# Masked attention stage: normalising the probabilities before they are turned, instead of dividing the heads' output by sums from a product with ones

## What is computed

```python
def _L0_xattn_ref(query, keys, values, mask, Wq, bq, Wk, bk, Wv, bv, Wo, bo):
    q = (query @ Wq.T + bq).reshape(N, Lq, HEADS, HEAD_DIM).transpose(0, 2, 1, 3)
    ...
    energy = jnp.einsum('bhqd,bhkd->bhqk', q, k)
    energy = jnp.where(mask[:, None, None, :] == 0, jnp.float32(-1e+20), energy)
    attention = jax.nn.softmax(energy / np.sqrt(HEAD_DIM), axis=-1)
    out = jnp.einsum('bhqk,bhkd->bhqd', attention, v)
    out = out.transpose(0, 2, 1, 3).reshape(N, Lq, EMBED)
    return out @ Wo.T + bo
x = x + _L0_xattn_ref(_layernorm(x), ctx_1024, ctx_1024, mask_BxS2_ik0, ...)
```

## Time and profile before

| | us |
|---|---|
| median of 3 runs (3192.03 to 3195.54) | 3193.3 |
| profiled execution | 3187.25 |
| its span, first to last instruction | 3185.5 |
| busy over the span: TensorE matmul | 3017.8 |
| VectorE | 2186.4 |
| ScalarE | 2009.2 |
| GpSimd | 941.1 |

### The profile page before, as it was taken

One profiled execution on the slowest core, in us unless ns is written; L12 is line 12 of the kernel. 1 busy time (PEld: TensorE's weight loads), 2 busy tenths in 40 slices (PEclk: granted clock), 3 DMA queues, 4 the chain that ended last, 5 costly groups with the idle time before them and its releaser, 6 DMA issues. The chain is left out here.

```text
span 3185.5 us, 88343 instructions
## 1 busy us (share of the span) xinstructions
PE 3017.8 (95%) x34369; PEld 2466.6 (77%) x34369; DVE 2186.4 (69%) x5188; ACT 2009.2 (63%) x3697; POOL 941.1 (30%) x812
## 2 busy tenths in 40 slices
PE   8999999979999999999979999999999999799999
PEld 7888888857877877877868888788788787564798
DVE  5777777766666666666644788778778877567543
ACT  5777777757767767677743677676666766332444
POOL 3444444337656555555630000000000000111210
PEclk9999999989999999999989999999999999899899
DMA  2111111237888888888885111111111110552000
GB/s 86 47 46 46 46 46 46 57 52 128 151 141 150 151 137 146 152 145 148 156 188 173 35 42 49 55 42 49 56 42 42 54 36 19 179 163 77 7 21 27
DMA packets 643036, 273.37 MB, mean 86 GB/s; under 512 B 549387, under 2 KB 617952, under 8 KB 642736
## 3 DMA queue, kind: packets, MB, share of 16 engines
q1 hardware_dynamic: 613168, 225.13, 33.6%
q10 hardware_dynamic: 29568, 44.05, 4.2%
HBM read 113.37 MB, written 21.50 MB: 42 GB/s over the span
## 5 line engine op out<-in xcount | busy, mean ns | idle before, releaser
L1310 POOL TENSOR_TENSOR front_parts<-wide_prob,front_parts 128x1024 f16<-128x1024 f32 x256 | 549.1, 2146 | 377.5 <-ACT front_parts L1536 318.6
L1629 DVE TENSOR_REDUCE wide_row_max<-wide_score 128x1 f32<-128x1024 f32 x256 | 312.6, 1221 | 167.4 <-PE wide_score L1348 166.5
L1348 PE MATMUL wide_score<-wide_kT,wide_qT 128*128 128x512 f32 x1536 | 414.3, 405 | 4.9 <-ACT wide_prob L1524 3.3
L1524 ACT ACTIVATE wide_prob<-wide_score,wide_neg_max 128x1024 f32<-128x1024 f32 x256 | 285.2, 1114 | 157.3 <-DVE wide_neg_max L1632 151.0
L886 ACT ACTIVATE mask_prob<-mask_prob,mask_row_min 128x256 f32<-128x256 f32 x512 | 232.0, 503 | 161.7 <-DVE mask_row_min L966 161.7
L1348 PEld LDWEIGHTS wide_score<-wide_kT,wide_qT 128*128 128x128 f32 x1536 | 277.5, 190 | 66.0 <-issue 8.9
L1536 ACT ACTIVATE front_parts<-wide_prob 128x1024 f16<-128x1024 f32 x256 | 269.8, 1054 | 16.8 <-ACT wide_prob L1524 8.3
L2472 DVE TENSOR_REDUCE cell_row_max<-cell_score 128x8 f32<-128x512 f32 x192 | 131.0, 682 | 148.5 <-PE cell_score L2097 146.6
L117 POOL TENSOR_TENSOR cell_var_eps<-cell_mean_var,const_eps 128x4 f32<-128x4 f32 x8 | 1.6, 202 | 651.9 <-DVE cell_mean_var L111 651.9
L1364 PE MATMUL wide_turn<-front_probT,wide_v 128*128 128x256 f16 x1536 | 189.5, 273 | 2.5 <-DMA front_probT<-front_parts 2.5
L1364 PE MATMUL wide_pv<-front_probT,wide_v 128*128 128x256 f16 x1536 | 189.9, 273 | 0.5 <-DMA front_probT<-front_parts 0.5
(11 more groups left out here) (364 smaller groups left out, 6845.6 us busy)
## 6 DMA issues: line engine op xcount, KB each, us to landing
cell_w_stage<-cell_weights ACTq DMA_DIRECT2D x24, 768.0 KB, 6.1
mask_ctx<-in_ctx SPq DMA_DIRECT2D x32, 512.0 KB, 3.9
ctx_ctx<-in_ctx SPq DMA_DIRECT2D x32, 512.0 KB, 4.2
mask_mask<-in_mask_BxS_ik SPq DMA_DIRECT2D x32, 256.0 KB, 4.0
front_probT<-front_parts SPq DMA_TRANSPOSE x512, 3.2
cell_w_stage<-in_L_ffn_We ACTq DMA_DIRECT2D x24, 256.0 KB, 2.7
cell_w_stage<-in_L_ffn_Wo ACTq DMA_DIRECT2D x24, 256.0 KB, 3.1
front_x_all<-in_x SPq DMA_DIRECT2D x32, 128.0 KB, 2.0
```

The costliest lines, as they stand in the source:

```text
L1310: pool.tensor_tensor(parts[:, s % 2, LO, :], prob[:, s % 2, :], parts[:, s % 2, HI, :], ALU.subtract).then_inc(part_lo, 1)
L1348: mm = pe.matmul(score[:, s % 2, half * 512:(half + 1) * 512], qT[:, u_par, a, s * P:(s + 1) * P], kT[:, par, b, half * 512:(half + 1) * 5 ...
L1524: act.activation(prob[:, s % 2, :], score[:, s % 2, :], ACT.Exp, bias=neg_max[:, s % 2:s % 2 + 1], scale=SHARP, accum_out=row_sum[:, u_par ...
L1629: dve.tensor_reduce(row_max[:, one], score[:, s % 2, :], AX.X, ALU.max).then_inc(max_found, 1)
```

## The change

What it does, part by part:

1. ScalarE's exponentials write their row sums (`accum_out`) to `row_sum`. VectorE inverts the two sums of a step as soon as its exponentials are done (`invert(u, t)`, [128, 2]). GpSimd multiplies the step's two probability tiles by them in place (`scale_probs`), and turn_probs waits for that in place of the exponentials.
2. `attend` has only its half with v. `pick` handles values alone and writes `oT`, now with two buffers, directly; `scale_o`, the reciprocal over [128, 256] and the tile of ones are gone. `project_o` waits for pick.
3. The orders change. TensorE: scores(u, 1) goes ahead of turn_ctx(1), and scores(n, 0) ahead of turn_probs(6). ScalarE: exp(4) goes ahead of copy_ctx(1) and copy_turned(2), exp(5) ahead of copy_turned(3), exp(6) and exp(7) one place ahead; copy_turned(6) moves to VectorE. VectorE: the minima 4 to 7 stand earlier among the other work, ln_stats is moved up, pick(u, 0) down. GpSimd: the mask reading, the two spreads and the normalisation stand between the scales.

In the order of the file: turn_probs, attend, TensorE's body, exp, ScalarE's body.

```diff
-            pe.wait_ge(exp_done, g + 1)
+            pe.wait_ge(prob_scaled, g + 1)
...
-            for what in (VALUE, SUM):
...
+            for kt in range(KT):
+                for r in range(ROW):
+                    p = hf * ROW + r
+                    mm = pe.matmul(heads[r * ROWS:(r + 1) * ROWS, hf * P:(hf + 1) * P], v[:, k, b * KT + kt, p * ROWS:(p + 1) * ROWS],
+                                   probT[:, p // 2, p % 2, kt, :], start=(kt == 0), stop=(kt == KT - 1))
...
             turn_probs(u, 1)
+            scores(u, k, 1)
             if not last:
                 turn_ctx(nxt, 1 - k, 1)
-            scores(u, k, 1)
...
-                project_o(u - 1)
+                project_o(u - 1, 1 - k)
+            if not last:
+                scores(nxt, 1 - k, 0)

             turn_probs(u, 6)
             attend(u, k, 2)
             if not last:
-                scores(nxt, 1 - k, 0)
                 project_v(nxt, 0, None)
...
-                ins = act.activation(prob[:, b, p, :], prob[:, b, p, :], ACT.Exp, bias=row_min[:, b, p:p + 1], scale=-1.0)
+                ins = act.activation(prob[:, b, p, :], prob[:, b, p, :], ACT.Exp, bias=row_min[:, b, p:p + 1], scale=-1.0,
+                                     accum_out=row_sum[:, b, p:p + 1])
...
             copy_turned(u, 1)
+            exp(u, 4)
             if not last:
                 copy_ctx(u + 1, 1)
             copy_turned(u, 2)
-            exp(u, 4)
+            exp(u, 5)
             copy_turned(u, 3)
-            exp(u, 5)
             if not last:
                 copy_q(u + 1)
+            exp(u, 6)
+            if not last:
                 copy_k(u + 1, 1 - k, 0)
-            exp(u, 6)
+            exp(u, 7)
             if not last:
                 copy_k(u + 1, 1 - k, 1)
             copy_turned(u, 5)
-            exp(u, 7)
-            copy_turned(u, 6)
```

More of the change, by code:

```diff
@@ L594, in normalise @@
             pool.tensor_tensor(xn[:, :], xn[:, :], rstd[:, :].to_broadcast([P, D]), ALU.mult).then_inc(xn_ready, 1)
[L596 to L622, removed]
+        def read_mask(u, k, b):
+            if b == 0:
+                pool.wait_ge(mask_loaded[k], loads(u, k))
+                if later(u):
+                    pool.wait_ge(min_found, (u - 1) * STEPS)
+                pool.tensor_tensor(pool_cell[:, 2 + k:3 + k], mhalf[:, 0:1], mhalf[:, 0:1], ALU.add)
+            ins = pool.tensor_scalar(shut[:, k, b].rearrange("p t r -> p r t"),
+                                     mask_sb[:, k, b * CTX:(b + 1) * CTX].rearrange("p (r t) -> p r t", t=KT), 0.0, SHUT,
+                                     ALU.is_equal, ALU.mult)
+            if b == 1:
+                ins.then_inc(shut_ready, 1)
@@ L629, in body @@
         def body(u, k, first, last):
+            scale_probs(u, 1)
             if not last:
-                read_mask(u + 1, 1 - k)
-            if not first:
-                scale_o(u - 1)
+                read_mask(u + 1, 1 - k, 0)
+            scale_probs(u, 2)
             if not last:
[L635 to L638, removed]
+                read_mask(u + 1, 1 - k, 1)
+            scale_probs(u, 3)
+            scale_probs(u, 4)
+            if not last:
+                spread(u + 1, 1 - k, HI)
+            scale_probs(u, 5)
+            if not last:
+                spread(u + 1, 1 - k, LO)
+            scale_probs(u, 6)
+            if not last and has_second(u):
+                inverse_std(u + 2)
+                normalise(u + 2, k)
+            scale_probs(u, 7)
+            if not last:
+                scale_probs(u + 1, 0)
             add_bias(u, k)
-        pool.wait_ge(pool_set, 4)
+        pool.wait_ge(pool_set, 3)
         inverse_std(0)
         normalise(0, 0)
-        read_mask(0, 0)
+        for b in range(2):
+            read_mask(0, 0, b)
         pool.wait_ge(prep_step, 1)
-        spread(0, 0)
+        for part in (HI, LO):
+            spread(0, 0, part)
         pool.wait_ge(w_loaded, 16 * W_LOADS)
@@ L651, in _ @@
         pool.wait_ge(prep_step, 3)
+        scale_probs(0, 0)
         units(pool, body)
-        scale_o(UNITS - 1)
     @block.tensor
@@ L839, in _ @@
         pe.wait_ge(y_ready, UNITS - 1)
-        project_o(UNITS - 1)
+        project_o(UNITS - 1, 1)
     @block.scalar
@@ L1028, in body @@
         def body(u, k, first, last):
+            invert(u, 1)
             copy_turned(u, 0)
             find_min(u, k, 3)
+            invert(u, 2)
+            if not last and has_second(u):
+                ln_stats(u + 2, k)
             if not first:
-                pick(u - 1, 1)
-                invert(u - 1)
+                pick(u - 1, 1 - k, 1)
             if not last:
-                for h in range(DH):
-                    ctx_lo(u + 1, h)
+                ctx_lo(u + 1, 0)
             find_min(u, k, 4)
+            invert(u, 3)
+            if not last:
+                ctx_lo(u + 1, 1)
             find_min(u, k, 5)
+            invert(u, 4)
+            find_min(u, k, 6)
             if not last:
                 q_lo(u + 1)
-            find_min(u, k, 6)
+            invert(u, 5)
+            find_min(u, k, 7)
             copy_turned(u, 4)
@@ L1044, in body @@
                 k_lo(u + 1, 1 - k, 0)
-            pick(u, 0)
-            find_min(u, k, 7)
+            invert(u, 6)
             if not last:
                 k_lo(u + 1, 1 - k, 1)
-            if not last and has_second(u):
-                ln_stats(u + 2, k)
+            invert(u, 7)
+            pick(u, k, 0)
             if not first:
@@ L1053, in body @@
             if not last:
-                for t in range(3):
-                    find_min(u + 1, 1 - k, t)
+                find_min(u + 1, 1 - k, 0)
+            copy_turned(u, 6)
+            if not last:
+                find_min(u + 1, 1 - k, 1)
+                invert(u + 1, 0)
+                find_min(u + 1, 1 - k, 2)
         dve.wait_ge(pool_set, 3)
@@ L1073, in _ @@
         ln_stats(1, 1)
-        for t in range(3):
-            find_min(0, 0, t)
+        find_min(0, 0, 0)
+        find_min(0, 0, 1)
+        invert(0, 0)
+        find_min(0, 0, 2)
         units(dve, body)
-        pick(UNITS - 1, 1)
-        invert(UNITS - 1)
+        pick(UNITS - 1, 1, 1)
         finish(UNITS - 1, 1)
```

58 lines of the change are left out of this document (25 added, 33 removed).

## The result

| | us |
|---|---|
| before, median of 4 runs beside it (3192.03 to 3200.01) | 3194.42 |
| after, median of 4 runs (3217.16 to 3224.02) | 3221.60 |
| ratio, with its 95% interval | 1.0081 (1.0063 to 1.0098) |
| profiled execution of after | 3222.03, its span 3220.3 |

The change makes the kernel 0.8% slower, inside the predicted range and 7 us above the predicted 3215. The forecast's account of the unit held. Two things did not: TensorE's clock, which the forecast let stay at its full level, and the belief that TensorE alone bounded the kernel before.

A forecast was written before the change was run, and what follows sets the result against it. The prediction took TensorE's own stream as the bound until the next queue is late. Period +0.80 us over 31 steps (+24.8), start +0.3, end -3.5: +21.6 on 3187.25, 3208.8; median 6.05 higher, 3215; range 3190 to 3240.

The forecast's parts named there:

- The front: Stretch from turn_probs(0) to turn_probs(3): a chain through find_min(4), exp(4) and copy_ctx(1) takes 7.41 us, 1.57 more than 5.84.
- The rest of the unit: From turn_probs(3) to the next turn_probs(0): 13.67 us falls to 12.47, plus 0.43 of wait, 12.90.
- The period: One unit of the masked stage: 7.41 + 12.90 = 20.31 us, 0.80 more than 19.51; +24.8 over 31 steps.
- The sums of work: Work per unit by engine: TensorE 17.4 us, ScalarE 14.7 to 16.4, VectorE about 13.8, GpSimd 15.5.
- The removed products: Products with ones in four attends a unit, 1.84 us of TensorE; those of attend(3) and attend(0) fall into idle time.
- Prices: Assumed costs of new operations: accumulator read 0.09 us, GpSimd scale 1.04, small reciprocal at most 0.16.
- TensorE's sum rules: Faster rival: front 4.8 us, period 17.3, total 3121; decides below a front of 6.61 us; chance 0.11.
- The clock: Rival: TensorE's clock falls to 0.89 through idle stretches of 2 us in every unit, giving 3262; chance 0.05.
- The start: Start of the masked stage: the first turn_probs waits for a scale, +0.3 us.
- The end: End of the masked stage: reciprocal and scale_o path gone, last scale and invert added, last unit shorter; -3.5 us.
- The wait for k_lo(1): TensorE's wait before scores(n,0), now ahead of turn_probs(6): 3.27 against 2.84, so 0.43 us added a unit.
- rival of an even end: Front 0.6 to 0.7 us shorter than walked, period about 19.65, 3190 to 3200; chance 0.13.

The follow-up runs named there:

- the kept products: The change, with attend(3) and attend(0) doing a second, unread product as large as the removed one with ones; 3206.29 us, ratio 1.0042 to before.
- the order undone in one place: The change, with exp(4) back behind copy_turned(2) and exp(5) behind copy_turned(3) on ScalarE; 3184.64 us, ratio 0.9969 to before.
- the second rewoven order: The change's operations in new queue orders, with scale(1), scale(2), exp(n,2) and exp(n,3) run before the unit begins; 3144.37 us, ratio 0.9846 to before.
- the change with the later scores: The change, with scores(n,0) back behind attend(2) on TensorE; 3225.66 us, ratio 1.0112 to before.
- the half scales: The change, with each GpSimd scale covering only the first half of the keys; 3222.59 us, ratio 1.0089 to before.

## Why the prediction was right, and where it was not

- **The front**: 7.41 us predicted; 297.67 to turn_probs(3) at 305.12 is 7.45. Every link holds, exp(3) to copy_ctx(0) and exp(4) to copy_ctx(1) with 1.00 each. VectorE's idle time before ctx_lo(1) was to be about 1.5 and is 1.56; TensorE's before turn_probs(3) nearly 2 and is 1.83 by the matmul row, 2.06 by the weight load's.
- **The rest of the unit**: 12.90 predicted, 305.12 to 317.85 is 12.73. Inside it, k1 to scores(n,0) was walked at 3.27 and takes 3.24.
- **The period**: 20.31 predicted, 20.18 and 20.33 in the ordinary units, 20.25 in the mean. Over 31 steps that is 23 us of the predicted 24.8.
- **The sums of work** held as well. By the shares of the 300 us above, a unit has 13.7 us of VectorE (13.8 predicted), 14.9 of ScalarE (14.7 to 16.4), 15.5 of GpSimd (15.5) and 17.6 of TensorE (17.4).
- **The removed products**: that those of attend(3) and attend(0) lie in idle time was argued, and the kept products show it, by an unchanged period.
- **Prices**: read 0.09 in pitch (303.37 to 303.46, and 0.36 a unit when four of them leave the chain), scale 1041 ns, small reciprocal 0.16. The figure of the Trainium skill (GPSIMD Engine Reference, section 3.1), 4497 ns for 2048 columns, made the scale an estimated 1.12 us; the trace has 1041 ns for it, 7% less.
- **TensorE's sum rules** decided below a front of 6.61. With the order undone in one place the front is 6.51 and the kernel is indeed faster than before, by 9 us; in the second rewoven order it is 5.00, and the kernel gains 49. The rival's condition was named rightly, its 3121 was 23 us too far: at a period of 18.03 TensorE's loads still wait 0.82 us ahead of scores(n,0) and 0.49 ahead of turn_probs(3), where some 0.2 is usual:

```profile
301.81 0.42 PEld L763 LDWEIGHTS mask_turn<-const_ident,mask_prob 128*128 128x128 f32 x4
...
306.81 0.42 PEld L763 LDWEIGHTS mask_turn<-const_ident,mask_prob 128*128 128x128 f32 x4 [0.49 <-issue]
...
314.05 0.81 PEld L749 LDWEIGHTS mask_score<-mask_kT,mask_q_diag 32*128 32x128 f32 x24 [0.82 <-issue]
```

- **The clock**: the step that failed. It was a rival of 0.05 with a clock of 0.89 throughout. What came is between: the full clock in most units and 1.4 us more in one of six, 7 us in the stage. The prediction had compared with a stretch of 80% and one gap of 1.6 us, and took that for a full clock. It named the idle stretches of 2 us in every unit as what spoke against, but counted the fall as all or nothing, so no term of the sum stands for a fall in single units. The rule of the Trainium skill (TensorE: Matmul & The Clock Gate, Part 1) that inactivity halves the array's clock agrees with the rows at 119 to 122 us, where the granted clock is 0.50 behind an idle stretch; that it made the whole rival the outcome doesn't hold, since the same idle time left the clock at 1.00 in five units of six.
- **The start**: 0.3 predicted, 2.8 measured: the first of the steady units' turns of x stands at 31.21, before at 28.38. The granted clock between 18 and 24 us is 0.51, and was 1.00 before. The same delay comes without the change and its absence with it: the kernel before with half of the ones product has the clock at 0.51 there and this point at 30.85, and the change with the later scores has 1.00 and 28.05. So most of the 2.8 goes with the clock at the start of an execution and not with the change:

```profile
18.00:24.00 6.00, 5.70 (x18) 4.89 (x19) 1.48 (x5) 0.62 (x2) 2.04 (x2) 0.51 0.50 153
18.00:24.00 6.00, 6.00 (x19) 5.09 (x20) 1.03 (x3) 0.63 (x2) 2.04 (x2) 0.51 0.47 135
18.00:24.00 6.00, 4.61 (x24) 3.65 (x24) 2.33 (x5) 2.00 (x4) 2.04 (x2) 1.00 0.46 139
```

(In this order: after, the kernel before with half of the ones product, the change with the later scores.) What ends the clock's first low stretch sooner or later was not tested.
- **The end**: -3.5 predicted. From the last turn_probs(0) to the next stage's first load it is 17.6 us (665.87 to 683.44), before 22.4 (632.57 to 655.00): -4.9. The term was too small by 1.4.
- **What bounds the kernel before**: "TensorE's own stream is the bound, and whatever leaves it is worth time" is refuted by the half ones product. The second half of that sentence, that it holds only until the next queue is late, was the right one, and the next queue was late at once. The price of 1.84 us for the removed products was right as TensorE's work, not as time.
- **The wait for k_lo(1)**, 0.43 of the sum, was sized rightly (the load waits 0.68, of which some 0.2 is usual) but wrongly taken for a cost on its own: taken away it gives 0.37 *more*, for behind it scale(6), pick and copy_turned(6) are as late. The prediction had scale(6) "some 1 us early" in the order of the change, which it is only while scores(n,0) stands ahead. Its rival of an even end counts a part of this wait into the front, where it doesn't stand.

By pieces: 23 for the periods, 7 for the clock, 2.8 for the start, -4.9 for the end is 27.9 of the 28.4 us by which the stage ends later. The forecast had 21.6 for the same, and its misses partly cancel: the clock and the start came on top, the periods and the end were less. That it lies only 7 us below the median owes something to that.

## What to carry to other kernels

When a change moves work off a full engine and reorders the queues at the same time, walk the chain of hand-overs at its tightest place link by link; sums of busy time would have given 3121 here, the walk gave 3215. A producer placed earlier in a queue (exp(4)) delays whatever stood there (copy_turned(2)), and one swap in one queue, find_min(4) with ctx_lo(0), changed the sign. Before believing a releaser, look when it ended: a name on an idle stretch may be a condition met a microsecond ago, and to halve that operation is a cheap test.

## What the runs showed of the hardware

- The granted clock of TensorE can fall to half in the middle of a stage with TensorE 86% busy. In after it did so once in six units, some 122.9 us apart, each time within the idle time before turn_probs(3), and cost 1.4 us. Products that nothing reads, put near that idle time, did away with all the falls; the kernel was 15 us faster, of which the trace shows 8.
- The length of that idle time (by the weight load's row) doesn't decide alone how many units are hit. Of 30 units, 5 were long at 2.06, 6 at 2.07 with the half scales, 3 at 2.07 with the later scores, 10 at 1.88 without the row sums, none at 1.63 with the products kept, one at 1.29 and 1.05 in turn, none at 1.12. Which units are hit is not settled.
- GpSimd's multiplication of 128x512 took 1.04 us with VectorE idle throughout (the scale at 303.08) and 1.04 us with VectorE busy throughout (the one at 309.12, beside a find_min, a copy out of PSUM and k_lo(0)).
